# A stack of conditioned layers: the order of each step's waits, the loading of a branch condition, and new orders of steps on all engines

## The reference, cut to what matters

```python
x = rotate_pairs(x, theta[b], phi[b])                      # layer 0
h = gelu(x @ Wi[e[b]] + bi[e[b]])                          # layer 1: one of 8 experts, 256 -> 1024 -> 256
x = layernorm(h @ Wo[e[b]] + bo[e[b]] + x) * gamma[e[b]] + beta[e[b]]
# layer 2: one of three branches, chosen by c[b]
#   c == 0 or 1: gelu(x @ w1) @ w2       c == 2: gelu(gelu(x @ w1_sr) @ w2_sr) @ w3_sr, w1_sr 256 -> 512
x = layernorm(x + branch(x, c[b])) * gamma2 + beta2
# layer 3: adaptive layernorm, attention with 16 heads of 16 columns, feed-forward 256 -> 1024 -> 256
x = layernorm(x) * (1 + scale[t[b]]) + shift[t[b]]
s = q @ k.T / 4 + bias[b]                                  # bias: 16 x 256 x 256 per batch, from HBM
s = where(mask[b], -inf, s)
x = x + softmax(s) @ v @ Wo3 + bo3
y = layernorm(x) * g2 + beta2_3
x = x + gelu2(y @ W1 + b1) @ W2 + b2
```

## Time and profile before

| what | us |
|---|---|
| three runs | 2075.09, 2072.59, 2075.19; median 2075.09 |
| span of the profiled execution | 2069.5 |
| PE busy with matmuls | 1921.3 (93%), 14354 matmuls |
| PE busy with loads of weights | 1676.1 (81%) |
| DVE busy | 1590.7 (77%) |
| ACT busy | 1376.7 (67%), of it table loads 437.5 |
| POOL busy | 252.4 (12%) |
| DMA | 356.12 MB, mean 172 GB/s |
| chain that ended last | PE 76%, DVE 12%, issue 5%, ACT 4%, DMA 1% |

### The profile page before, as it was taken

The page is one execution under the profiler, slowest core; times in us unless marked ns, Lnnn a source line. Parts: engine busy times, 40 slices in busy tenths (PEclk is TensorE's granted clock), DMA queues, the critical chain, the costliest instruction groups (busy, mean ns, idle before and its releaser), DMA issues.

```text
span 2069.5 us, 43614 instructions
## 1 busy us (share of the span) xinstructions
PE 1921.3 (93%) x14354; PEld 1676.1 (81%) x14354; DVE 1590.7 (77%) x5373; ACT 1376.7 (67%) x2210; POOL 252.4 (12%) x361
## 2 busy tenths in 40 slices
PE   5789999999999999999999999999999999999786
PEld 4668888888888888888888888888888888788676
DVE  4577877787887788887777888778888877877774
ACT  3376677677667677767767767766776776666443
POOL 1111111011111011111001111101111110111100
PEclk9799999999999999999999999999999999999998
DMA  6655555665565566654555655556665546653450
GB/s 221 202 172 167 187 153 158 186 203 182 183 178 148 156 202 192 196 181 154 154 187 183 195 172 179 164 174 201 189 196 181 177 146 177 216 159 118 133 153 11
DMA packets 222311, 356.12 MB, mean 172 GB/s; under 512 B 29523, under 2 KB 120147, under 8 KB 222068
## 3 DMA queue, kind: packets, MB, share of 16 engines
q1 hardware_dynamic: 222068, 352.99, 56.0%
HBM read 294.12 MB, written 58.79 MB: 171 GB/s over the span
## 4 chain that ended last, share of the span: by engine, by line
PE 76%; DVE 12%; issue 5%; ACT 4%; DMA 1%; ACTq 0%; SPq 0%; POOL 0%; DVEq 0%; POOLq 0%
PE pD L471 51%; PE pX L687 11%; PE pS L471 9%; DVE bias_ring L1178 4%; PE pC L471 3%; DVE bias_ring L975 3%; PE pC L709 1%; DVE x_nat L972 1%; ACT L777 1%; DVE crossed L972 1%; ACT gelu_out L777 1%; ACT probs L777 1%; ACT hid L777 1%; DVE res L978 0%; DVE y_nat L978 0%
## 5 line engine op out<-in xcount | busy, mean ns | idle before, releaser
L1178 DVE CUSTOM_DVE_ANT_0 bias_ring<-pS,bias_ring 128x256 f32<-128x256 f32 x1024 | 389.5, 418 | 200.3 <-PE pS L471 197.4
L777 ACT ACTIVATE probs<-pX 128x512 f32<-128x512 f32 x512 | 304.6, 595 | 225.1 <-PE pX L687 222.8
L777 ACT ACT_TABLE_LOAD x341 | 437.5, 1283 | 18.9 <-PE pD L471 12.0
L687 PE MATMUL pX<-ident,bias_ring 128*128 128x128 f32 x2048 | 321.2, 280 | 61.4 <-DVE bias_ring L975 49.3
L687 PEld LDWEIGHTS pX<-ident,bias_ring 128*128 128x128 f32 x2048 | 228.9, 141 | 147.2 <-issue 95.9
L975 DVE TENSOR_SCALAR bias_ring<-bias_ring,row_max 128x256 f32<-128x256 f32 x1024 | 321.8, 357 | 18.3
L471 PE MATMUL pS<-k_stack,q_stack 96*128 96x256 f32 x1024 | 304.5, 379 | 0.0
L471 PE MATMUL pD<-x,raw 128*128 128x256 f32 x1024 | 246.4, 384 | 3.0 <-ACT gelu_out L777 1.0
L471 PE MATMUL pD<-raw,gelu_out 128*128 128x256 f32 x1024 | 237.6, 379 | 0.0
L471 PEld LDWEIGHTS pS<-k_stack,q_stack 96*128 96x128 f32 x1024 | 197.9, 193 | 19.8
L471 PEld LDWEIGHTS pD<-x,raw 128*128 128x128 f32 x1024 | 188.2, 191 | 31.8 <-issue 9.7
(11 more groups left out here) (148 smaller groups left out, 3663.4 us busy)
## 6 DMA issues: line engine op xcount, KB each, us to landing
bias_ring<-in_fside SPq DMA_DIRECT2D x512, 256.0 KB, 4.4
raw<-in_experts SPq DMA_DIRECT2D x128, 512.0 KB, 4.7
q_spill<-hid SPq DMA_DIRECT2D x96, 256.0 KB, 3.4
k_spill<-hid SPq DMA_DIRECT2D x96, 256.0 KB, 3.4
q_stack<-q_spill SPq DMA_DIRECT2D x128, 192.0 KB, 4.3
k_stack<-k_spill SPq DMA_DIRECT2D x64, 384.0 KB, 5.6
norm<-in_expert_rows SPq DMA_DIRECT2D x32, 384.0 KB, 4.1
x_nat<-in_x SPq DMA_DIRECT2D x32, 256.0 KB, 3.1
```

Of the source, the lines that this page charges most:

```text
L687: last = e.transpose(pX[:, k, t * P:(t + 1) * P], bias_ring[:, u % NBIAS, t, k * P:(k + 1) * P], ident[:, :])
L777: return e.activation(o, i, func, bias=bias, scale=scale)
L1178: e.tensor_tensor_reduce(bias_ring[:, n, t, :], pS[:, t, :], bias_ring[:, n, t, :], 1.0, -3.4e38, ALU.add, ALU.max, row_max[:, n, t:t + 1] ...
```

## The change

Four things change. In most steps with several waits the wait that comes last by rights is named first, so that it sits on the step's instruction and the others on semaphore instructions ahead of it. Waits that an earlier step of the same engine has already passed are left out (in `scores`, `values`, `hidden`). The condition c of a batch is loaded once at the start of `front(b)` on PE, ACT and DVE, in place of three times on PE and twice on the two others, and the waits move into the branches behind it. And the tables FIRST, ORDER and LAST have new orders for all five engines. No arithmetic changes.

The core of the diff (of the tables the lines of ORDER, and of the waits those that the prediction speaks of):

```diff
 ORDER = {
-    "PE": "hhfhhfhhhhfrrhhfrhhfhhhghhhghhrhhghhhhhhgrgrhhgghhrgghhrfhhhhfrrhhfr",
-    "ACT": "rhrhrfhrrhfrrrhfrhfrfhhfhrffrhfhhrhghhghhhgrhghg",
-    "DVE": "hrhfrhrfhrhfhhrfhrfhghrhhhrhhfhfrhrhrfhrfghrfg",
+    "PE": "fhhhfhhhfrrhhfrhhfhhhghhhghhrhhghhhhhhgrgrhhgghhgrghhrfhhhhfrrhhfrhh",
+    "ACT": "rfhhrrfrhrrfhrfhfrhfrhfhfrfhhrhghghhhhgrhghghrrh",
+    "DVE": "hfrhrfhrhfhhrgfhrfhhhhrhrhhfhfrhrhrfhfrghrfghr",
...
                 def turn_input():
+                    e.wait_ge(sem["x0_made"], b + 1)
                     if b:
                         e.wait_ge(sem["act_narrow"], 3 * b)
                         e.wait_ge(sem["act_deep"], 9 * b)
-                    e.wait_ge(sem["x0_made"], b + 1)
                     turned(WIDE, x_nat).then_inc(sem["x0_turned"], 1)
...
                 def branch_in():
                     xa = [(xa_hi[:, k, :], xa_lo[:, k, :]) for k in range(K)]
-                    low = sem["x1_lo"], b + 1
-                    e.wait_ge(sem["x1_hi"], b + 1)
-                    c = e.value_load(idx[0:1, 1, b:b + 1])
+                    high, low = (sem["x1_hi"], b + 1), (sem["x1_lo"], b + 1)
                     with e.If(c == 2):
+                        e.wait_ge(*high)
                         for i in range(2):
...
+                c = e.value_load(idx[0:1, 1, b:b + 1])
+                e.wait_ge(sem["y1_made"], b + 1)
                 if b:
                     e.wait_ge(sem["v_made"], 2 * b)
-                e.wait_ge(sem["y1_made"], b + 1)
                 turned(BANK["y1"], y_nat).then_inc(sem["y1_turned"], 1)
...
                 def turn(h):
                     u = u0 + h
-                    if u:
-                        e.wait_ge(sem["exp_made"], u)
                     for t in range(T):
                         e.wait_ge(sem["subtracted"], T * u + t + 1)
+                        if u and t == 0:
+                            e.wait_ge(sem["exp_made"], u)
...
                 def deep(i):
                     name, first = (("L2_cond_b1_sr", 0), ("L2_cond_b1_sr", 2), ("L2_cond_b2_sr", 0))[i]
                     e.wait_ge(sem["pe_deep"], 3 * b + i + 1)
+                    if i == 0:
+                        hid_free()
+                    if i == 2:
+                        e.wait_ge(sem["dve_deep"], 3 * b + 1)
                     gelu_and_hi(BANK[f"deep{i}"], i % 2, i % 2, [col(name, first + n) for n in range(2)], "act_deep", 9 * b + 3 * i)
...
                 with e.If(c == 2):
-                    e.wait_ge(sem["dve_deep"], 3 * b + 1)
                     deep(2)
```

More of the change, by code:

```diff
@@ L690, in values @@
                 def values(q):
+                    e.wait_ge(sem["exp_made"], 4 * q + 4)
                     if q:
@@ L695, in values @@
                         e.wait_ge(sem["dve_zeros"], 1)
-                    e.wait_ge(sem["exp_made"], 4 * q + 4)
-                    e.wait_ge(sem["v_made"], 2 * (q // 4 + 1))
+                    if q % 4 == 0:
+                        e.wait_ge(sem["v_made"], 2 * (q // 4 + 1))
                     for k in range(K):
@@ L733, in tail @@
             def tail(b):
+                e.wait_ge(sem["ctx_made"], 4 * b + 4)
                 if b:
                     e.wait_ge(sem["gated"], 4 * b)
-                if not b:
+                else:
                     e.wait_ge(sem["dve_folded"], 1)
                     e.wait_ge(sem["dve_w"], runs_before(NW))
-                e.wait_ge(sem["ctx_made"], 4 * b + 4)
                 turned(TAIL, ctx_nat).then_inc(sem["ctxT"], 1)
                 yield
+                xc_parts = [(xc_hi[:, k, :], xc_lo[:, k, :]) for k in range(K)]
+                e.wait_ge(sem["ctx_hi"], b + 1)
                 if b:
                     e.wait_ge(sem["out_made"], b)
-                xc_parts = [(xc_hi[:, k, :], xc_lo[:, k, :]) for k in range(K)]
-                e.wait_ge(sem["ctx_hi"], b + 1)
                 to_natural(SUM_T, "Wo", 0, xc_parts, (sem["ctx_lo"], b + 1)).then_inc(sem["wo"], 1)
@@ L752, in hidden @@
                 def hidden(m2):
-                    e.wait_ge(sem["x3_lo"], b + 1)
                     e.wait_ge(sem["hid_seeded"], 4 * b + m2 + 1)
+                    if m2 == 0:
+                        e.wait_ge(sem["x3_lo"], b + 1)
                     to_turned(TAIL, "W1", FF, 2 * P * m2, xc_parts, start=False).then_inc(sem["w1"], 1)
@@ L841, in front, with hid_free @@
                 yield
-                if b:
-                    e.wait_ge(sem["dma_spill"], 96 * b)
-                e.wait_ge(sem["wide_out"], 4 * b + 4)
-                if not b:
-                    e.wait_ge(sem["dve_cols"], 1)
-                c = e.value_load(idx[0:1, 1, b:b + 1])
+                def hid_free():
+                    if b:
+                        e.wait_ge(sem["dma_spill"], 96 * b)
+                    e.wait_ge(sem["wide_out"], 4 * b + 4)
+                    if not b:
+                        e.wait_ge(sem["dve_cols"], 1)
                 with e.If(c == 2):
@@ L1060, in summed, with scaled @@
                 last.then_inc(sem[which + "_var"], 1)
-            def scaled(srcs, dst, which, n, gamma, beta, scaled_, made_):
+            def scaled(srcs, dst, which, n, gamma, beta, scaled_, made_, others=()):
                 e.wait_ge(sem[which + "_var"], n + 1)
+                for other, count in others:
+                    if count > 0:
+                        e.wait_ge(sem[other], count)
                 for t in range(T):
@@ L1071, in scaled, with normalise @@
                 step(last, made_)
-            def normalise(srcs, dst, which, n, made_):
+            def normalise(srcs, dst, which, n, made_, free):
                 e.wait_ge(sem[which + "_rstd"], n + 1)
+                if free[1]:
+                    e.wait_ge(sem[free[0]], free[1])
                 for t in range(T):
@@ L1216, in tail @@
                 yield
-                if b:
-                    e.wait_ge(sem["ffn_turned"], b)
-                normalise(rows, ffn_in, "tail", b, "ffn_in_made")
+                normalise(rows, ffn_in, "tail", b, "ffn_in_made", ("ffn_turned", b))
                 yield
```

99 lines of the change are left out of this document (50 added, 49 removed).

## The result

| | before | after |
|---|---|---|
| median of five runs | 2075.09 us | 2011.97 us |
| span of the profiled execution | 2069.5 us | 2010.2 us |
| PE busy | 1921.3 us | 1906.5 us |
| PE idle | 148.2 us | 103.7 us |

The changed kernel takes 0.9698 of the time (95% interval 0.9686 to 0.971): 63 us less, where 53 were forecast. 59.3 us of it are in the spans. The other 3.8 us are chance: in every run of either kernel whose span is on record the time is 1.7 to 1.9 us above the span, so the profiled execution of before, at a span of 2069.5 us, was 3.8 us faster than the median. The 5.6 us between its span and the median, of which the text ahead speaks as what lies around the span, are these two together. In the later rounds the kernel before had medians of 2073.4 to 2073.9 us; against them the change wins about 62 us.

A forecast was written before the change was run, and what follows sets the result against it. PE was taken to bound the kernel, with only its 148.2 us of idle time reachable. Terms 16 + 23 - 5 + 9 + 4 + 5 - 7 = 45 us, plus 8 at the ends, made 53: 2075.1 - 53 = 2022 us, range 2012 to 2034.

The forecast's parts named there:

- The condition loaded ahead, 16 us: Ahead of branch_in on PE: load and branches run before x1_hi comes; 16 us won, bounds 0 and 16.5.
- rotate, 23 us: rotate earlier on DVE ends the waits before the transposes of x_nat and head 13; 23 us won, bounds 0 and 23.
- Minus 5 for head 11's maxima: On DVE, rotate ahead of the branch's low part may delay head 11's maxima; 5 us lost, bounds 0 and 31.
- plus 4 for head 10's exponential: On ACT, head 10's exponential now stands ahead of two steps; 4 us won, bounds 0 and 8.
- The third branch, 9 us: ACT's table load ends before PE is done, so branch_out and an exponential come earlier; 9 us won, bounds 0 and 9.
- Late waits on the instruction, 5 us: Each late wait put on the step's own instruction saves 0.10 us; 5 us won, bounds -3 and 8.
- Minus 7 for the product with W1: x3_lo and the seed come later, so the first product with W1 starts 0.27 us late; 7 us lost, bounds 0 and 64.
- The ends, 8 us: The 6 batches outside the middle of the run, with waits partly of other kinds; 8 us won.
- half of it comes back: Rival, 2048 us, chance 0.27: waits on DVE and ACT only shift and rotate's 23 us fail to come.
- Slower: Rival, 2084 us, chance 0.05: x3_lo makes the product with W1 2.4 us late in each batch, 62 us lost.
- The load only moves: Rival, 2075 us, chance 0.03: the earlier load of the condition stops the sequencer as the branch did; no change.
- More than the sum: Rival, 2006 us, chance 0.13: the ends give 19 us in place of 8 and head 11's charge falls away.

The follow-up runs named there:

- e4_cond: Changed kernel with branch_in on PE as before: wait for x1_hi first, then load the condition, then branch; 2028.1 us.
- e1_waits: Kernel before with all the edits of waits and of the condition's loads, but its own old tables of order; 2047.2 us.
- e3_rotate: Changed kernel with rotate put back on DVE, behind the maxima of head 12, in batches 5 to 29; 2066.7 us.
- e9_rot_pool: Changed kernel with both rotate on DVE and POOL's addition to x_nat put back in their old places, batches 5 to 29; 2041.8 us.
- e10_pool: Changed kernel with only POOL's addition to x_nat put back, behind the tail's root, batches 5 to 29; 2015.1 us.
- e6_deep: Changed kernel with ACT's last stage of the third branch waiting as before, for TensorE's product ahead of the table load; 2022.6 us.
- e5_turn: Changed kernel with the waits of a head's transposes in their old order, the exponential first, then the subtraction; 2011.4 us.
- e7_gelu0: Changed kernel with ACT's first gelu of the experts' part put back behind head 14's exponential, batches 5 to 29; 2010.2 us.
- e8_norm: Changed kernel with DVE's normalising of the heads' values moved one step later, behind the maxima of heads 6, 10 and 14; 2003.4 us.

## Why the prediction was right, point by point

The direction and the size held: 2012 against 2022, at the lower bound of the range (2012 to 2034). The sum was 10 us short, and that it comes so near is in part luck: charges of 12 us (head 11, W1) came only to 3, and late waits and ends, forecast with 5 and 11.5 us, to 2 and 5.

- *The condition loaded ahead, 16 us.* Right: 0.70 us per batch, 26 batches 18 us (of the 27 waits in the row, 25 with 11.4 us stood ahead of branch_in). Taken alone it is 14 to 17 (e4_cond 0.52 us per batch, e1_waits 0.64 at branch_in). The bound of 0, a branch that costs the same everywhere, is excluded.
- *rotate, 23 us.* Right: 26 x 0.90 = 23.4 as a difference, 26 x 0.86 = 22 by experiment (27 by its medians). But a condition was missing: with the new order of DVE and POOL, rotate in its old place costs 2.15 us per batch (e3_rotate against after), since POOL's addition to x_nat meets the subtractions of head 13.
- *Minus 5 for head 11's maxima, plus 4 for head 10's exponential.* Head 11 won 0.23 us per batch, 6 us, where the two terms made -1. The maxima came only 0.13 us behind the scores, and rotate costs head 11 no more than 0.06 us per batch (e3_rotate; 0.05 in e9_rot_pool against e10_pool), 1.5 us. The charge was one step that failed: rotate mostly fills time in which DVE had nothing to do.
- *The third branch, 9 us.* Right, 8.9 us for 26 batches (e6_deep), 11 for the whole kernel. Of the 25 waits for probs 8 stood at head 12 and 17 at head 11, not 7 and 18 as I had it, which moves less than 0.5 us between this term and that of head 10.
- *Late waits on the instruction, 5 us.* Wrong in size: the start moved by 0.09 us as forecast (0.044 us behind the semaphore in place of 0.135), but the same heads waited 0.07 us longer for their second half. -0.08 us per batch in the account, nothing in e5_turn.
- *Minus 7 for the product with W1.* Wrong by what was not read: POOL's addition had doubled the making of ffn_in, 1.68 us against 0.73, and it moved away with the change. DVE got 0.95 us back in just the chain that I charged. With POOL's step put back, 0.22 us of the charge of 0.27 come true (e10_pool); as it is, the product is 0.07 us longer, 2 us.
- *gelu ahead of head 14's exponential, 0.* Right: -0.28 and +0.37 us; e7_gelu0 gives 0.05.
- *The ends, 8 us, 11.5 with the two batches that the window held more.* 5.0 us in the two traces, which is also what such traces differ by at the start: too much, as far as can be told.
- q and head 0, 0.14 us per batch, were in no term. The 3.8 us by which the profiled execution of before was faster than its median were in none either, and no term could have held them.

Of the rivals, "half of it comes back" rested on rotate's 23 us, and they came. "Slower" by x3_lo had its mechanism, worth 0.2 us with POOL's old order, far from the 2.0 at which it would have decided. "The load only moves" is out by e4_cond. "More than the sum" had one ground right, no charge for head 11, and the ends, its other, gave less than forecast. In the forecast's signs one failed: no new wait stood ahead of the product with W1.

Not settled: how much of e8_norm's gain before batch 4 is the edit, which applies there too, and how much is chance. The five spans of after differ by up to 2.5 us (2008.0 to 2010.5), and no experiment takes the ends apart. Which steps make up the 15 us that come only with both parts is read from the accounts, not tested one by one. Why head 5 takes 0.09 us longer in e1_waits stays open as well.

## What to carry to other kernels

Put a sequencer's loads and branches, and a table load, ahead of the wait that ends last: here a load and a branch ahead of a product cost 0.6 us per batch, and a table load behind a wait 1.2 us per use. Price a moved step by who runs beside it as well, on POOL above all: the same rotate was worth 0.9 or 2.1 us per batch, by where POOL's addition stood. An end of the program in which little runs beside each other answers to other edits than the middle. Where two engines hand a head to and fro, removing one delay only shows the next; try such edits in pairs, and read the time of a batch as well as the total.

## What the runs showed of the hardware

- A subtraction on DVE from SBUF to SBUF that starts behind POOL's addition stands still while it runs and ends 0.15 us behind it: 1.62 us in place of 0.62 for the pair of head 13, 1.68 in place of 0.73 for that of ffn_in, 1.36 us each time for the one held up. POOL's own addition took 1.40 to 1.42 us then, against 1.27.
- When the semaphore that comes last is waited for by the instruction itself, the transposes' first weight load starts 0.04 us behind it and the matmul 0.044 (in the kernel before 821.449, 821.491 and 821.493); with a separate wait ahead it is 0.10 and 0.135 (826.205, 826.309 and 826.340). Winning this at a head's start was worth nothing in e5_turn.
- The condition's load took 302 ns in the median behind a wait and 490 ns when issued ahead of other work, at no cost to PE.
